# A decoder layer on one NeuronCore: sums of tokens shared with GpSimd and spread over steps 3 to 9, and four banks for the plain query tiles

## The reference, cut to what matters

```python
q = (query @ wq).reshape(bs, sq, 32, 128).transpose((0, 2, 1, 3))      # wq: 512 x 4096
k = (key @ wk).reshape(bs, sk, 8, 1, 128)                               # each key head serves four query heads
v = (value @ wv).reshape(bs, sk, 8, 1, 128)
q = _apply_rope(q, 0); k = _apply_rope(k, 0)
raw = jnp.einsum('bhqd,bhkd->bhqk', q, k) / sqrt(128)
attn = jax.nn.softmax(raw + mask, axis=-1)
out = jnp.einsum('bhqk,bhkd->bqhd', attn, v)                            # then out @ wo, 4096 x 512
```

## Time and profile before

| | us |
|---|---|
| runs | 873.24, 875.88, 876.21 |
| median | 875.88 |
| profiled execution: its own time | 875.86 |
| its span in the profile | 874.1 |
| TensorE busy | 844.3 (97%) |
| VectorE busy | 677.0 (77%) |
| GpSimd busy | 565.7 (65%) |
| ScalarE busy | 453.8 (52%) |

### The profile page before, as it was taken

One profiled execution on the slowest core, in us unless ns is written; L12 is line 12 of the kernel. 1 busy time (PEld: TensorE's weight loads), 2 busy tenths in 40 slices (PEclk: granted clock), 3 DMA queues, 4 the chain that ended last, 5 costly groups with the idle time before them and its releaser, 6 DMA issues.

```text
span 874.1 us, 15787 instructions
## 1 busy us (share of the span) xinstructions
PE 844.3 (97%) x4676; PEld 700.2 (80%) x4676; DVE 677.0 (77%) x2114; ACT 453.8 (52%) x1516; POOL 565.7 (65%) x538
## 2 busy tenths in 40 slices
PE   7999999999999897999999999999999999999996
PEld 6788888788877676888888888888888787778884
DVE  5466888888876998888898889888888967546646
ACT  4336988778752434454555555545554565440320
POOL 4625866766675676678787787878785877455002
PEclk9999999999999999999999999999999999999998
DMA  8679998967760211122222222122221331000001
GB/s 278 261 230 216 221 195 172 181 155 149 191 212 34 87 43 35 56 71 64 65 66 71 63 65 64 64 64 64 65 63 65 108 116 46 24 13 25 25 2 47
DMA packets 82581, 88.27 MB, mean 101 GB/s; under 512 B 8129, under 2 KB 61633, under 8 KB 82497
## 3 DMA queue, kind: packets, MB, share of 16 engines
q1 hardware_dynamic: 82496, 87.26, 37.1%
HBM read 64.13 MB, written 23.07 MB: 100 GB/s over the span
## 4 chain that ended last, share of the span: by engine, by line
PE 78%; DVE 11%; issue 5%; ACT 3%; POOL 1%; DMA 1%; POOLq 0%; DVEq 0%; ACTq 0%; SPq 0%
PE banks L35 62%; PE banks L1279 6%; PE banks L1262 3%; PE banks L752 2%; PE banks L770 1%; PE banks L743 1%; DVE C_t L1403 1%; DMA stage<-wv_dram 1%; ACT B_prob L681 1%; DVE B_prob L840 1%; DVE C_t L1398 1%; DVE C_t L1404 1%; PE banks L122 1%; PE banks L367 1%; POOL B_wv L171 1%
## 5 line engine op out<-in xcount | busy, mean ns | idle before, releaser
L35 PE MATMUL banks<-C_wo,C_o 128*128 128x512 f32 x768 | 192.2, 399 | 1.7 <-issue 1.2
L35 PEld LDWEIGHTS banks<-C_wo,C_o 128*128 128x128 f32 x768 | 139.6, 188 | 30.6 <-ACT C_o L1165 1.6
L1165 ACT ACTIVATE C_o<-banks 128x512 fp32r<-128x512 f32 x64 | 38.3, 599 | 201.9 <-PE banks L35 201.9
L1563 POOL TENSOR_TENSOR C_q<-C_t,C_t 128x512 f32<-128x512 f32 x64 | 84.7, 1324 | 52.8 <-DVE C_t L1404 52.2
L681 ACT ACTIVATE B_prob<-B_prob,B_top 128x128 f32<-128x128 f32 x256 | 99.6, 392 | 26.1 <-DVE B_top L840 26.1
L1145 ACT ACTIVATE C_prob<-C_prob,C_top 128x128 f32<-128x128 f32 x256 | 99.3, 391 | 16.4 <-DVE C_top L1491 15.7
L593 POOL TENSOR_TENSOR B_prob<-B_prob,B_rden 128x512 f32<-128x512 f32 x64 | 67.7, 1059 | 36.9 <-DVE B_rden L849 36.9
L1570 POOL TENSOR_TENSOR C_prob<-C_prob,C_rden 128x512 f32<-128x512 f32 x64 | 72.4, 1131 | 18.4 <-DVE C_rden L1501 18.4
L35 PE MATMUL banks<-xT,C_block 128*128 128x512 f32 x288 | 71.2, 389 | 0.0
L840 DVE CUSTOM_DVE_ANT_0 B_prob<-banks,causal 128x128 f32<-128x128 f32 x256 | 58.9, 286 | 14.5 <-issue 13.3
L1279 PE MATMUL banks<-C_kv,C_q 128*128 128x128 f32 x512 | 67.8, 275 | 1.4 <-DVE C_top L1491 1.4
(11 more groups left out here) (186 smaller groups left out, 2048.3 us busy)
## 6 DMA issues: line engine op xcount, KB each, us to landing
C_kv<-cross_kv_d SPq DMA_DIRECT2D x64, 192.0 KB, 2.3
cross_kv_d<-B_v_out SPq DMA_DIRECT2D x16, 512.0 KB, 4.0
stage<-wq_dram SPq DMA_DIRECT2D x32, 256.0 KB, 2.6
stage<-wo_dram SPq DMA_DIRECT2D x32, 256.0 KB, 2.6
heads_q<-heads_q_d SPq DMA_DIRECT2D x96, 64.0 KB, 3.8
heads_k<-heads_k_d SPq DMA_DIRECT2D x96, 64.0 KB, 3.8
heads_q_d<-cT SPq DMA_DIRECT2D x8, 512.0 KB, 2.9
heads_k_d<-cT SPq DMA_DIRECT2D x8, 512.0 KB, 2.9
```

The lines of the kernel that those rows point to most:

```text
L35: mm = eng.matmul(out, stationary[i], moving[j], start=first and n == 0, stop=last and n == len(PASSES) - 1)
L1563: eng.tensor_tensor(self.query(r), by_batch(t1), by_batch(t2), ALU.add).then_inc(self.s_sum, 1)
```

## The change

Two things change. First, `pj` gets two more banks (1 and 5), used by tiles 8 to 15 in the order 1, 5, 6, 7: `project` of such a tile waits until tile r-4 has been read, not r-2. The first block product, which takes bank 1, waits until 14 tiles have been rotated. Second, six of the sums of tokens (x12, x22 and the raw T4, two pieces each) go from VectorE's steps 3, 4, 5 to GpSimd's steps 3, 4, 5 (`token_parts`), placed behind `tile_sum` and ahead of `blocks_lo` and `piece_lo`. The high parts on ScalarE are spread over steps 5, 6, 7, 8 in the order T1, T2, T4, T3, and the low parts on VectorE (`token_lo`) over the end of step 7 (T1), the starts of steps 8 (T2) and 9 (T3), and the end of step 9 (T4). ScalarE copies the first block product (`copy_products` of step 7) in step 8 behind the turned probabilities, no longer at the end of step 7.

```diff
+        self.pj += [chip.bank(1), chip.bank(5)]
...
     def scalar(self, eng, n):
         if n == 2:
             self.pieces_hi(eng, 1)
+        if n == self.AT + 1:
+            self.copy_products(eng, self.AT)
         if self.live(n, 2):
...
         self.T_hi(eng, n)
-        self.copy_products(eng, n)
+        if n != self.AT:
+            self.copy_products(eng, n)
...
     def T_hi(self, eng, n):
-        for i in {6: (1, 2), 7: (3, 4)}.get(n, ()):
+        if n in self.HI_AT:
+            i = self.HI[self.HI_AT.index(n)]
...
+    def pj_of(self, r):
+        return self.pj[r % 2 if r < 2 * self.Q else (r + 2) % 4]
...
-            wait(eng, self.s_sin, r - 1)
+            wait(eng, self.s_sin, r - 1 if r < 2 * self.Q else r - 3)
...
-            mm = product(eng, self.pj[r % 2], [t[:, c * P:(c + 1) * P] for t in self.w[j]],
+            mm = product(eng, self.pj_of(r), [t[:, c * P:(c + 1) * P] for t in self.w[j]],
...
         if phase == 0:
             wait(eng, self.s_e, k)
+            if k == 0:
+                eng.wait_ge(self.s_sin, self.PLAIN - 2)
...
+    HI, HI_AT = (1, 2, 4, 3), (5, 6, 7, 8)
...
     def token_sums(self, eng, n):
...
             if n == 3:
-                eng.tensor_tensor(raw(1, c), part(0, 0, c), part(0, 1, c), ALU.add).then_inc(self.s_x, 1)
-                if c == 0:
-                    eng.wait_ge(self.before.s_tp, self.before.NS)
-                eng.tensor_tensor(by_batch(self.x12[c][:, :]), part(1, 0, c), part(1, 1, c), ALU.add).then_inc(self.s_x, 1)
+                eng.tensor_tensor(raw(1, c), self.part(0, 0, c), self.part(0, 1, c), ALU.add).then_inc(self.s_x, 1)
             if n == 4:
-                eng.wait_ge(self.s_x, 4)
-                eng.tensor_tensor(raw(1, c), by_batch(self.x12[c][:, :]), raw(1, c), ALU.subtract).then_inc(self.s_t, 1)
-                eng.tensor_tensor(by_batch(self.x22[c][:, :]), part(1, 0, 2 + c), part(1, 1, 2 + c), ALU.add)\
-                   .then_inc(self.s_x, 1)
+                eng.wait_ge(self.s_x, c + 1)
+                eng.wait_ge(self.s_parts, c + 1)
+                eng.tensor_tensor(raw(1, c), x12[c], raw(1, c), ALU.subtract).then_inc(self.s_t, 1)
             if n == 5:
-                eng.wait_ge(self.s_x, 6)
-                eng.wait_ge(self.s_t, 2)
-                eng.tensor_tensor(raw(2, c), by_batch(self.x22[c][:, :]), raw(1, c), ALU.subtract).then_inc(self.s_t, 1)
-                eng.tensor_tensor(raw(4, c), part(0, 0, 2 + c), part(0, 1, 2 + c), ALU.add).then_inc(self.s_x, 1)
+                eng.wait_ge(self.s_t, c + 1)
+                eng.wait_ge(self.s_parts, c + 3)
+                eng.tensor_tensor(raw(2, c), x22[c], raw(1, c), ALU.subtract).then_inc(self.s_t, 1)
...
-        for i in {7: (1, 2), 8: (3, 4)}.get(n, ()):
-            for c in range(2):
-                eng.wait_ge(self.s_Thi, 2 * i - 1 + c)
-                eng.wait_ge(self.s_t, 6)
-                eng.tensor_tensor(self.T_part(i, 1, c), raw(i, c), self.T_part(i, 0, c).bitcast(F32), ALU.subtract)\
-                   .then_inc(self.s_Tlo, 1)
+    def token_lo(self, eng, i):
+        for c in range(2):
+            eng.wait_ge(self.s_Thi, 2 * self.HI.index(i) + 1 + c)
+            eng.wait_ge(self.s_t, {1: 4, 2: 6, 3: 8, 4: 6}[i])
+            eng.tensor_tensor(self.T_part(i, 1, c), self.T_sum(i, c), self.T_part(i, 0, c).bitcast(F32), ALU.subtract)\
+               .then_inc(self.s_Tlo, 1)
...
     def vector(self, eng, n):
         tiles = self.tiles(n)
+        if n == self.AT + 1:
+            self.token_lo(eng, 2)
+        if n == self.AT + 2:
+            self.token_lo(eng, 3)
         self.add_products(eng, n - 1)
...
         self.token_sums(eng, n)
+        if n == self.AT:
+            self.token_lo(eng, 1)
+        if n == self.AT + 2:
+            self.token_lo(eng, 4)
...
     def gpsimd(self, eng, n):
         for r in self.tiles(n):
             self.tile_sum(eng, r)
+        self.token_parts(eng, n)
...
+    def token_parts(self, eng, n):
+        if n == 3:
+            eng.wait_ge(self.rows.s_lo, B)
+            eng.wait_ge(self.before.s_tp, self.before.NS)
+        for c in range(2):
+            if n == 3:
+                eng.tensor_tensor(by_batch(self.x12[c][:, :]), self.part(1, 0, c), self.part(1, 1, c), ALU.add)\
+                   .then_inc(self.s_parts, 1)
+            if n == 4:
+                eng.tensor_tensor(by_batch(self.x22[c][:, :]), self.part(1, 0, 2 + c), self.part(1, 1, 2 + c), ALU.add)\
+                   .then_inc(self.s_parts, 1)
+            if n == 5:
+                eng.tensor_tensor(self.T_sum(4, c), self.part(0, 0, 2 + c), self.part(0, 1, 2 + c), ALU.add)\
+                   .then_inc(self.s_parts, 1)
```

More of the change, by code:

```diff
@@ L998, in __init__ @@
         self.s_x, self.s_t, self.s_Thi, self.s_Tlo = sem("x"), sem("t"), sem("Thi"), sem("Tlo")
+        self.s_parts = sem("parts")
         self.s_pj, self.s_cos, self.s_sin, self.s_sum = sem("pj"), sem("cos"), sem("sin"), sem("sum")
@@ L1377, in source @@
         if r < self.PLAIN:
-            return self.pj[r % 2]
+            return self.pj_of(r)
         return (self.beta, self.gamma, self.delta, self.h[:, :])[self.pair(r)[1]]
@@ L1440, in tile_from_products, with part @@
         eng.wait_ge(self.s_u, 3 * k + i + 1)
+    HI, HI_AT = (1, 2, 4, 3), (5, 6, 7, 8)
     T_RAW = {(1, 0): 1, (1, 1): 2, (2, 0): 3, (2, 1): 4, (4, 0): 5, (4, 1): 6, (3, 0): 7, (3, 1): 8}
+    def part(self, half, lo, c):
+        return self.rows.xT[:, 4 * half:4 * half + 4, lo, c, :].bitcast(F32)
     def token_sums(self, eng, n):
-        part = lambda half, lo, c: self.rows.xT[:, 4 * half:4 * half + 4, lo, c, :].bitcast(F32)
-        raw = self.T_sum
+        raw, x12, x22 = self.T_sum, [by_batch(t[:, :]) for t in self.x12], [by_batch(t[:, :]) for t in self.x22]
@@ L1462, in token_sums @@
-                eng.wait_ge(self.s_t, 2)
-                eng.tensor_tensor(raw(2, c), by_batch(self.x22[c][:, :]), raw(1, c), ALU.subtract).then_inc(self.s_t, 1)
-                eng.tensor_tensor(raw(4, c), part(0, 0, 2 + c), part(0, 1, 2 + c), ALU.add).then_inc(self.s_x, 1)
+                eng.wait_ge(self.s_t, c + 1)
+                eng.wait_ge(self.s_parts, c + 3)
+                eng.tensor_tensor(raw(2, c), x22[c], raw(1, c), ALU.subtract).then_inc(self.s_t, 1)
             if n == 6:
-                eng.wait_ge(self.s_x, 8)
@@ L1467, in token_sums @@
-                eng.wait_ge(self.s_t, 4)
+                eng.wait_ge(self.s_t, c + 3)
+                eng.wait_ge(self.s_parts, c + 5)
                 eng.tensor_tensor(raw(4, c), raw(4, c), raw(2, c), ALU.subtract).then_inc(self.s_t, 1)
@@ L1470, in token_sums @@
                 eng.wait_ge(self.s_pj, self.PLAIN)
-                eng.tensor_tensor(raw(3, c), by_batch(self.x22[c][:, :]), by_batch(self.x12[c][:, :]), ALU.subtract)\
-                   .then_inc(self.s_t, 1)
-        for i in {7: (1, 2), 8: (3, 4)}.get(n, ()):
-            for c in range(2):
-                eng.wait_ge(self.s_Thi, 2 * i - 1 + c)
-                eng.wait_ge(self.s_t, 6)
-                eng.tensor_tensor(self.T_part(i, 1, c), raw(i, c), self.T_part(i, 0, c).bitcast(F32), ALU.subtract)\
-                   .then_inc(self.s_Tlo, 1)
+                eng.wait_ge(self.s_parts, c + 3)
+                eng.tensor_tensor(raw(3, c), x22[c], x12[c], ALU.subtract).then_inc(self.s_t, 1)
+    def token_lo(self, eng, i):
[4 more added lines that the diff above has]
+               .then_inc(self.s_Tlo, 1)
     def minima(self, eng, n):
```

## The result

| | before | changed |
|---|---|---|
| first comparison, five runs each: median | 875.88 us | 867.18 us |
| ratio changed to before, 95% interval | | 0.9926 [0.9909, 0.9944] |
| the same two kernels again, on another occasion | 874.04 us | 869.63 us |
| ratio | | 0.9956 [0.9938, 0.9974] |
| and a third time | 875.61 us | 869.97 us |

A forecast was written before the change was run, and what follows sets the result against it. VectorE was taken to bound steps 4 to 6, with TensorE also waiting for a bank. The banks' 4.64 us, all other terms 0, took 875.86 to 871.22 us, forecast as 871.2, range 868.2 to 873.8.

The forecast's parts named there:

- The bank's waits: Steps 4 to 6: second tiles stop waiting for a bank, 10.31 us a step, 30.93 against 35.57, 4.64 us less.
- The lower figure: Steps 4 to 6: a more careful floor from TensorE's busy times, 4.1 us less; 4.64 was taken instead.
- VectorE's relief: Steps 3 to 5: two of four sums leave VectorE, which then needs 9.5 us a step, at worst 10.66.
- Six sums on GpSimd at no cost: Steps 3 to 5: GpSimd takes the sums, its results still 2.5 to 5 us early; cost 0 us.
- third rival: GpSimd becomes the bound, step 7 begins 1.4 us later than before, 877.3 us; chance 0.05.
- Step 8: VectorE's six instructions and 3.3 us of waiting stay, the clock falls, the step keeps 12.77 us: gain 0.
- first rival: The clock does not fall in step 8, 2.7 us less than forecast, 868.5 us; chance 0.14.
- Step 9 and 10 at no cost: Low parts of T3 and T4 move into step 9, turned_lo there at about 3.4 us; cost 0, at worst 0.5.
- the sum's silent one: Unstated in the sum 875.86 - 4.64: everything outside steps 3 to 10 keeps its time, 0 us.

The follow-up runs named there:

- e2: Kernel before with only the four banks for plain tiles, all sums of tokens still on VectorE; 871.98 us, ratio 0.9979 to before.
- e4: Changed kernel with each of the six moved sums made twice on GpSimd, same result; 874.12 us, ratio 1.0003 to before.
- e6: Changed kernel with T1's two low parts made by GpSimd in step 7 instead of VectorE; 868.07 us, ratio 0.9930 to before.
- e7: Changed kernel with the low parts of T1 and T2 made by GpSimd in step 7 instead of VectorE; 866.04 us, ratio 0.9902 to before.
- e5: Changed kernel with high parts, low parts and the first product's copy back where they were before; 870.36 us, ratio 0.9955 to before.
- e3: Changed kernel with two banks for plain tiles as before, six sums still on GpSimd; 871.74 us, ratio 0.9985 to before.
- e9: Changed kernel run again unchanged, on a third occasion beside before; 869.97 us, ratio 0.9938 to before.

## Why the prediction was right or wrong

**The bank's waits: right, and slightly small.** They were to go and steps 4 to 6 to take 10.31 us each. They take 10.22, because the 2.82 us for the second tile's 12 matmuls were taken behind a gap; without one, 24 take 5.44. The term is 4.91 us, not 4.64. The lower figure that I had kept from the busy time, 4.1, was wrong for the same reason.

**VectorE's relief: right.** The 11.67 us a step that banks alone would have left are in e2's last step, to the hundredth. The price of two sums was set too low: 2.39 us in step 4, but 3.23 in step 5 and 2.68 in step 6, against 2.4. As argued, TensorE didn't feel it: VectorE's first cosine of step 6 comes 1.28 us after the step's start and that of step 7 0.74 us. The Trainium skill ("SBUF — State Buffer", "Who interferes with whom") says that a VectorE instruction with two SBUF inputs contends with a GpSimd instruction that reads SBUF, for a port pair that only one can hold. The trace agrees in that both sums of step 5 took longer beside GpSimd (1536 and 1770 ns, against 693 alone) while the rotations stay at 0.68 to 0.69 us; whether the second was blocked wholly or in part, these durations don't tell.

**Six sums on GpSimd at no cost: right.** The queue that was followed had normalisations 3, 4 and 5 at 302.0, 314.5 and 324.0; with the 1.3 us by which this profile lies earlier they are at 302.4, 314.7 and 324.3. The reserve is 2.1 us at step 6's start, and e4 shows what lies beyond it: all of its 4.71 us. The third rival's mechanism exists, then, beyond that reserve; its 877.3 us stood for a still longer queue than e4's, which gave 874.12.

**Step 8: the chain right, the clock half right.** The idle time stayed at 3.25 us behind the same six instructions, and e6 and e7 show that they make it. Spreading the low parts was worth nothing, as forecast (e5). The first rival had the clock not fall at all; in fact it falls in each profile of the changed kernel, but stays down for 3.4 us in two of them and for 6.8 in the third, with 11.70, 11.77 and 12.76 us for the step. That this rival's 868.5 us is the nearest to the first median, 867.18, is luck: what it names didn't happen. (The range gives that rival as 868.2, its own sum is 868.5.)

**Step 9 and 10 at no cost: right, with less room than was said.** 6.81 us, and 7.50 for step 10. But T3's low parts waited 1.88 us for ScalarE, and the low part of the turned probabilities ended 3.9 us after the step's start, where 3.4 had been expected; the product with values began at 4.1. In e7, where step 8 is shorter, the same wait costs 0.81 us.

**The step that failed is the sum's silent one: that all outside steps 3 to 10 keeps its time.** The first profile of the changed kernel has 2.9 us less there (1.29 ahead of step 3, 1.62 behind step 10) and 1.27 less in steps 8 and 9. Most of it is in places where TensorE works at half pace for a varying time: at the start (0.95 us), around step 8's idle time and behind the gates; 0.4 us are in the waits of the self attention between 79 and 93 us. The trace of before showed the three slow places, and the runs of before that were known then differed by 3 us; I gave that spread to step 8 alone. In the later comparisons the gain is 4.4 and 5.6 us, around the 4.91 that the steps show in every profile of the changed kernel. So 4.91 us, 0.56%, is shown to be the change's own. The other 3.8 us of the first comparison no later one repeats: some 2.4 of them go with the runs' mean clock, by the estimate above, and the rest stays open. By them the first median is lower than forecast; that is the execution's luck and not a merit of the change.

## What to carry to other kernels

Where two limits lie close together (here the bank at 11.3 us a step and VectorE's queue at 11.7, over TensorE's 10.2), taking one away brings a third to a half of what both bring, and both have to go in one edit. Before work is moved to another engine, follow that engine's queue in time to each point at which somebody waits for it: here 2 us of reserve made six sums free, and doubling them took back the whole gain. And read the busy engine's rest: after the change the longest idle time was made of six instructions of VectorE while GpSimd stood idle beside them, and moving four of them brought another 0.5%.

## What the runs showed of the hardware

The same program on the same inputs had its clock at 0.50 for 3.4 or for 6.8 us at the same 3.25 us of idle time in step 8, which made the step 11.70 or 12.76 us long. The group behind the gates took 6.93 or 8.51 to 8.58 us in twelve profiles, nothing between; in the seven longer ones the clock stands at 0.50 for 3.4 us, though TensorE had no idle time ahead of it, only the small matmuls. The mean clock of whole runs went from 0.991 to 0.998, and their time by some 4 us with it. Runs of one kernel on one occasion differ by 1.3 us (the first five of the changed kernel) to 5.9 us (e3's twelve). A change worth 5 us of 870 needs several runs of both kernels side by side, their clocks beside their times, and the stretches of its own steps compared in the traces. After 2.05 us of idle time the clock was still seen to fall, one microsecond after work had begun again: 1.00 in 340 to 341, 0.72 and 0.50 in the next two in e6. In e9 it fell as late behind 3.25 us: work began again at 341.67, and the clock fell at 342.8.
